# Edge scatter spread over tables, layers and dot stage, with fused products, in a graph network on one core

## The reference

```python
src, dst, edge_attr_32            # edges sorted by dst; 32 features per edge
# L0: three graph attention layers of 4 heads
e = leaky_relu(alpha_s[src] + alpha_d[dst], 0.2)
alpha = softmax over the edges of one dst;  x = relu(segment_sum(alpha * h[src], dst) + b)
# L1: GIN      mlp(segment_sum(x[src], dst) + (1 + eps) * x), normed over nodes, relu
# L2: dot      exp_s = exp(clip(q[dst] . k[src], -10, 10)); attention with v, plus x
# L3: GINE     mlp(x + segment_sum(relu(x[src] + edge_attr @ We + be), dst)), normed, relu
```

## Time and profile before

| What | us |
|---|---|
| runs, lowest to highest | 6104.78 to 6120.56 |
| median of 3 runs | 6106.02 |
| the profiled execution | 6116.9 |
| its span, first to last instruction | 6114.9 |

### The profile page before, as it was taken

One profiled execution on the slowest core, in us unless ns is written; L12 is line 12 of the kernel. 1 busy time (PEld: TensorE's weight loads), 2 busy tenths in 40 slices (PEclk: granted clock), 3 DMA queues, 4 the chain that ended last, 5 costly groups with the idle time before them and its releaser, 6 DMA issues. The chain is left out here.

```text
span 6114.9 us, 65546 instructions
## 1 busy us (share of the span) xinstructions
PE 3509.3 (57%) x23361; PEld 2157.9 (35%) x23361; DVE 4003.1 (65%) x4450; ACT 2617.0 (43%) x4140; POOL 4178.9 (68%) x3306
## 2 busy tenths in 40 slices
PE   3211111211053778876889858888758783466664
PEld 2211111211052444443445434454433331344542
DVE  2644445554377999959998599996649995233323
ACT  1000000000043777876878857788029894122211
POOL 1888888888782788846888658887001488777773
PEclk6555555555566889998989979999879997777765
DMA  8222222222397889847998569996724243323222
GB/s 284 19 19 19 21 19 4 1 1 8 41 351 244 188 211 222 183 113 175 220 220 193 108 165 221 218 216 121 261 77 143 92 128 89 109 74 79 76 52 24
DMA packets 421587, 765.52 MB, mean 125 GB/s; under 512 B 178478, under 2 KB 257197, under 8 KB 417168
## 3 DMA queue, kind: packets, MB, share of 16 engines
q0 software_dynamic: 236096, 287.22, 30.9%
q1 hardware_dynamic: 166832, 432.41, 20.5%
q10 hardware_dynamic: 18336, 41.70, 2.0%
HBM read 632.89 MB, written 128.19 MB: 124 GB/s over the span
## 5 line engine op out<-in xcount | busy, mean ns | idle before, releaser
L325 POOL DMA_INDIRECT counts<-plcell_add,plcell_slot x806 | 1255.7, 1558 | 390.5 <-issue 222.8
L1629 POOL DMA_INDIRECT emxg<-xtab,emsrc x856 | 945.5, 1105 | 454.0 <-issue 260.2
L702 ACT ACT_TABLE_LOAD x1 | 1.3, 1283 | 1614.8 <-PE mtps L690 1614.8
L417 DVE TENSOR_REDUCE plnlow<-plsame 128x13 f32<-128x1664 bf16 x62 | 117.0, 1888 | 664.6 <-DMA counts<-plcell_add,plcell_slot 664.5
L372 PE MATMUL plpsR<-plpiece,plbefore 128*128 128x500 bf16 (+1 forms) x81 | 47.1, 582 | 820.7 <-DVE plranked L502 808.0
L1210 PE MATMUL ga0psE<-ident,ga0logit 128*128 128x128 f32 x2500 | 398.4, 298 | 192.2 <-DMA ga0logit<-log_counts 168.6
L1210 PE MATMUL ga1psE<-ident,ga1logit 128*128 128x128 f32 x2500 | 401.8, 301 | 148.4 <-DMA ga1logit<-log_counts 130.9
L1210 PE MATMUL ga2psE<-ident,ga2logit 128*128 128x128 f32 x2500 | 397.2, 299 | 148.9 <-DMA ga2logit<-log_counts 117.9
L1143 ACT ACTIVATE ga0prob<-ga0psE,ga0src_fifth 128x512 f32<-128x512 f32 (+1 forms) x700 | 405.3, 672 | 146.9 <-PE ga0psE L1210 146.2
L1143 ACT ACTIVATE ga1prob<-ga1psE,ga1src_fifth 128x512 f32<-128x512 f32 (+1 forms) x700 | 405.2, 671 | 145.1 <-PE ga1psE L1210 144.4
L1143 ACT ACTIVATE ga2prob<-ga2psE,ga2src_fifth 128x512 f32<-128x512 f32 (+1 forms) x700 | 405.5, 669 | 139.4 <-PE ga2psE L1210 138.6
(11 more groups left out here) (354 smaller groups left out, 8694.8 us busy)
## 6 DMA issues: line engine op xcount, KB each, us to landing
ga0logit<-log_counts POOLq DMA_DIRECT2D x88, 512.0 KB
ga1logit<-log_counts POOLq DMA_DIRECT2D x88, 512.0 KB
ga2logit<-log_counts POOLq DMA_DIRECT2D x88, 512.0 KB
counts<-plzeros SPq DMA_DIRECT2D x32, 1250.0 KB, 32.7
mthalf<-counts SPq DMA_DIRECT2D x50, 800.0 KB, 10.3
log_counts<-mtlogs SPq DMA_DIRECT2D x25, 1600.0 KB
ga0near<-log_counts SPq DMA_DIRECT2D x50, 800.0 KB
ga1near<-log_counts SPq DMA_DIRECT2D x50, 800.0 KB
```

What stands on the lines that cost most here:

```text
L325: nc.gpsimd.indirect_dma_start(counts[w][:, :], bass.IndirectOffsetOnAxis(ap=cell_slot[:, g % 2, j:j + 1], axis=0), cell_add[:, g % 2, j:j ...
L417: step(nc.vector.reduce_sum(nlow[:], same[:], axis=AX.X))
L702: nc.scalar.activation(logs[:, n % OUTS, q, :], ps[:, u % 3, 0:BW], ACT.Ln, bias=tiny[:, 0:1], scale=math.e).then_inc(log_made, 1)
L1629: nc.gpsimd.indirect_dma_start(xg[:, h, t, :], None, xtab[:, :], bass.IndirectOffsetOnAxis(ap=src[:, g, t:t + 1], axis=0)).then_inc(gather ...
```

## The change

The scatter groups are split anew: 8 beside the tables, 14 in each layer, and the last 12 in the block of L2 and L3, ahead of GpSimd's casts. The lists of slots and ends are loaded once for each stage instead of once for each group. SyncE's 54 row loads wait for the new scatters (semaphore `scattering`). In SyncE's queue the row loads of the first five visits stand ahead of the table's stores, and the first two early loads ahead of the last three early stores. Three products become scalar_tensor_tensor: the addition of half tables, the product with the counts (which takes over the clip's minimum) and the one-hot compare.

```diff
-TABLE_GROUPS = (0, 5)
-LAYER_GROUPS = ((5, 24), (24, 43), (43, 62))
+TABLE_GROUPS = (0, 8)
+LAYER_GROUPS = ((8, 22), (22, 36), (36, 50))
+DOT_GROUPS = (50, 62)
...
-                    nc.vector.tensor_tensor(cnt[:, n % OUTS], half[:, n % RING, 0], half[:, n % RING, 1], ALU.add).then_inc(summed, 1)
+                    nc.vector.scalar_tensor_tensor(cnt[:, n % OUTS], half[:, n % RING, 0], 0.0, half[:, n % RING, 1], ALU.add, ALU.add).then_inc(summed, 1)
...
+        pool.dma_start(slot[:], edges["slot"][:, first * G:last * G]).then_inc(tables_loaded, 16)
+        pool.dma_start(ends[:], edges["ends"][:, first * G:last * G, :]).then_inc(tables_loaded, 16)
...
-            pool.dma_start(slot[:, m, :], edges["slot"][:, g * G:(g + 1) * G]).then_inc(list_loaded[m], 16)
-            pool.dma_start(ends[:, m, :, :], edges["ends"][:, g * G:(g + 1) * G, :]).then_inc(list_loaded[m], 16)
...
+        scatter, _ = edge_scatter(nc, ctx, a, edges, "dots", *DOT_GROUPS)
...
+                sp.wait_ge(scattering, 1)
                 for g in range(SORTED_GROUPS):
...
+                sp.wait_ge(src_made, SORTED_GROUPS)
+                for i in range(ROWS):
+                    load_row(i)
                 sp.dma_start(xtab[FIRST * P:NP, :].rearrange("(t p) d -> p t d", p=P), x[:, FIRST:NT, :]).then_inc(filled, 16)
...
                 for g in range(EARLY_GROUPS):
+                    if g == EARLY_GROUPS - 3:
+                        load_early(0)
+                        load_early(1)
...
                 nc.gpsimd.iota(local_id[:], pattern=[[1, P]], base=0, channel_multiplier=0, allow_small_or_imprecise_dtypes=True).then_inc(id_made, 1)
+                for _ in scatter(pool):
+                    pass
+                pool.sem_inc(scattering, 1)
...
-                        nc.vector.tensor_scalar(w, w, EXP_LOW, EXP_HIGH, ALU.max, ALU.min).then_inc(clipped, 1)
+                        nc.vector.tensor_scalar(w, w, EXP_LOW, None, ALU.max).then_inc(clipped, 1)
...
-                        nc.vector.tensor_tensor(w, w, times(HEADS - first), ALU.mult).then_inc(prob_ready, 1)
+                        nc.vector.scalar_tensor_tensor(w, w, EXP_HIGH, times(HEADS - first), ALU.min, ALU.mult).then_inc(prob_ready, 1)
...
-                    nc.vector.tensor_tensor(same[:, v % M_BUFS, :, :], local_id[:].unsqueeze(1).to_broadcast([P, CT, P]),
-                                            row[:, i % ROWS, lo:lo + CT, ED:ED + 1].to_broadcast([P, CT, P]), ALU.is_equal).then_inc(same_ready, 1)
+                    nc.vector.scalar_tensor_tensor(same[:, v % M_BUFS, :, :], local_id[:].unsqueeze(1).to_broadcast([P, CT, P]), 0.0,
+                                                   row[:, i % ROWS, lo:lo + CT, ED:ED + 1].to_broadcast([P, CT, P]), ALU.add, ALU.is_equal).then_inc(same_ready, 1)
```

More of the change, by code:

```diff
@@ L757, in edge_scatter @@
     count = last - first
-    LISTS = 4
-    slot = sb("slot", [P, LISTS, G], i32)
-    ends = sb("ends", [P, LISTS, G, 2])
+    slot = sb("slot", [P, count * G], i32)
+    ends = sb("ends", [P, count * G, 2])
     feat = sb("feat", [P, STAGES, G, ED])
     stage = sb("stage", [P, STAGES, G, RW])
-    feat_cleared, staged = (sem(n) for n in ("feat_cleared", "staged"))
-    list_loaded = [sem(f"list_loaded{k}") for k in range(LISTS)]
+    tables_loaded, feat_cleared, staged = (sem(n) for n in ("tables_loaded", "feat_cleared", "staged"))
     feat_loaded = [sem(f"feat_loaded{k}") for k in range(STAGES)]
@@ L776, in load @@
         def load(i):
-            g, k, m = first + i, i % STAGES, i % LISTS
-            pool.dma_start(slot[:, m, :], edges["slot"][:, g * G:(g + 1) * G]).then_inc(list_loaded[m], 16)
-            pool.dma_start(ends[:, m, :, :], edges["ends"][:, g * G:(g + 1) * G, :]).then_inc(list_loaded[m], 16)
+            g, k = first + i, i % STAGES
             rows = feat[:, k, :, :].rearrange("p t k -> p (t k)")
@@ L789, in steps @@
         load(0)
+        pool.wait_ge(tables_loaded, 32)
         for i in range(count):
-            k, m = i % STAGES, i % LISTS
+            k = i % STAGES
             if i + 1 < count:
                 load(i + 1)
-            pool.wait_ge(feat_loaded[k], sum(loads(n) for n in range(k, i + 1, STAGES)))
-            pool.wait_ge(list_loaded[m], 32 * (i // LISTS + 1))
+            pool.wait_ge(feat_loaded[k], sum(loads(m) for m in range(k, i + 1, STAGES)))
             if i >= STAGES:
@@ L798, in steps @@
             nc.gpsimd.tensor_copy(stage[:, k, :, 0:ED], feat[:, k, :, :]).then_inc(staged, 1)
-            nc.gpsimd.tensor_copy(stage[:, k, :, ED:RW], ends[:, m, :, :]).then_inc(staged, 1)
+            nc.gpsimd.tensor_copy(stage[:, k, :, ED:RW], ends[:, i * G:(i + 1) * G, :]).then_inc(staged, 1)
             pool.wait_ge(staged, 2 * i + 2)
[L801 to L804, removed]
+            for t in range(i * G, (i + 1) * G):
+                nc.gpsimd.indirect_dma_start(edges["sorted"][:, :], bass.IndirectOffsetOnAxis(ap=slot[:, t:t + 1], axis=0),
+                                             stage[:, k, t - i * G, :], None).then_inc(scattered[k], 16)
+                yield t
         for k in range(STAGES):
@@ L1559, in dot_and_messages @@
         flat_a = ps_a.rearrange("p k c -> p (k c)")
[L1560 to L1561 removed]
+        be_loaded, we_cleared, we_loaded, column_loaded, need_loaded, need_met, scattering, zero_made, id_made = (
+            esem(n) for n in ("be_loaded", "we_cleared", "we_loaded", "column_loaded", "need_loaded", "need_met", "scattering", "zero_made", "id_made"))
         row_loaded = [esem(f"row_loaded{k}") for k in range(ROWS)]
@@ L1588, in _, with load_early @@
                 sp.dma_start(xtab[0:FIRST * P, :].rearrange("(t p) d -> p t d", p=P), y[:, 0:FIRST, :]).then_inc(x_stored, 16)
+                def load_early(g):
+                    if g < E_BUFS:
+                        sp.wait_ge(prob_used, TILES)
+                    else:
+                        sp.wait_ge(raw_ready, visit_end[visit_of[g - E_BUFS] + 1])
+                    sp.wait_ge(early_stored[g % XG], 16 * (g // XG + 1))
+                    sp.dma_start(early_in[:, g % E_BUFS].rearrange("p k d -> p (k d)"), edges["early"][g * P:(g + 1) * P, :]).then_inc(early_loaded[g % E_BUFS], 16)
                 for g in range(EARLY_GROUPS):
+                    if g == EARLY_GROUPS - 3:
+                        load_early(0)
+                        load_early(1)
                     for c in range(NCH):
@@ L1598, in _ @@
                         sp.wait_ge(feat_packed, i - ROWS + 1)
-                    sp.dma_start(row[:, i % ROWS, :, :].rearrange("p k w -> p (k w)"), sorted_groups[g]).then_inc(row_loaded[i % ROWS], 16)
-                    if g < EARLY_GROUPS:
-                        if g < E_BUFS:
-                            sp.wait_ge(prob_used, TILES)
-                        else:
-                            sp.wait_ge(raw_ready, visit_end[visit_of[g - E_BUFS] + 1])
-                        sp.wait_ge(early_stored[g % XG], 16 * (g // XG + 1))
-                        sp.dma_start(early_in[:, g % E_BUFS].rearrange("p k d -> p (k d)"), edges["early"][g * P:(g + 1) * P, :]).then_inc(early_loaded[g % E_BUFS], 16)
+                        load_row(i)
+                    if 2 <= g < EARLY_GROUPS:
+                        load_early(g)
             @block.gpsimd
```

3 lines of the change are left out of this document (2 added, 1 removed).

## The result

The changed kernel takes 6164.41 us (median of 4 runs, 6158.69 to 6169.34), the kernel before 6107.2 beside it (4 runs): a ratio of 1.0087 with a 95% interval of 1.0069 to 1.0106. It is slower by 57 us, 0.9%; 6176 was forecast, in a range of 6062 to 6250.

A forecast was written before the change was run, and what follows sets the result against it. VectorE and GpSimd were taken as both near their limit in the layers, and GpSimd's gather chain as setting the end. Tables +25, layers −75, dot stage +120 sum to +70: 6176 us, range 6062 to 6250.

The forecast's parts named there:

- the three terms: Whole kernel: +25 us in the tables, −75 in the three layers, +120 in the dot stage, summing to +70.
- Products: Three products as scalar_tensor_tensor: same durations as before and GpSimd not freed, 0 us.
- Tables: Table stage: three more scatter groups make GpSimd finish after VectorE's last product, +25 us, bounds 0 and +50.
- Layers: Three layers: five fewer groups each return somewhat over a third of VectorE's wait, −25 us per layer, −75 in all.
- The sign named for it was too strong: Layers of about 760 us, with TensorE's waits for masks down from 96 to 60 us or so.
- Dot stage: Twelve groups ahead of the gathers: first gather 184 us late, the gather chain ends 120 us later; bounds +51 and +174.
- The next step: Dot stage: 96 gathers move to where they take 1.25 instead of 1.924 us, so 184 us delay costs 120.
- First rows and early loads: SyncE's reordered loads fill part of the other engines' 116 us stillness, but gathers set the messages' pace: 0 us.
- The sign named for it failed: Before the messages: the other engines' 116 us of stillness shorter or filled, with no effect on the end.
- GpSimd paces the layers: Layers: TensorE's mask waits come from scatters, 60 us back per layer, 6071 us; decides from 48 per layer; chance 0.15.
- The layers return nothing: Layers: mask transfers, not their issue, hold TensorE, so no gain; sum +145, 6251 us; chance 0.12.

The follow-up runs named there:

- e1_products: The kernel before with only the three products as scalar_tensor_tensor and the clip without its minimum: 6109.9 us, ratio 0.9996 to the kernel before.
- e3_tables5: The changed kernel with 5 groups beside the tables, 15 in each layer, 12 in the dot stage: 6138.7 us, ratio 1.0040 to the kernel before.
- e7_layers5: The changed kernel with lists per group, 5 groups in the tables, 5 in each layer, 42 in the dot stage: 6701.0 us, ratio 1.0961 to the kernel before.
- e5_dots6: The changed kernel with 5 groups beside the tables, 17 in each layer, 6 in the dot stage: 6049.8 us, ratio 0.9890 to the kernel before.
- e10_hold: The kernel before with SyncE's 54 row loads held until 72 of 125 dot-stage tiles are added up, no scatters there: 6204.0 us, ratio 1.0144.
- e4_old_rows: The changed kernel with SyncE's old order, first rows behind the early stores, first two early loads behind the last three: 6160.8 us, ratio 1.0079 to the kernel before.

## Why the prediction was right

The result is 12 us below the forecast, and the three terms are there with the signs that were worked out. In the two profiled executions they add up to +50 instead of +70: the dot stage was taken 29 us too dear, the tables 7 too cheap. What follows are the sizes.

*Products: 0, right*, and alone as well (e1_products). In the changed kernel they take 1498 and 834 ns, with the scatters beside them. The rule of the Trainium skill that spoke against them (Vector Engine (DVE) Microarchitecture Reference, section 7: half throughput for two SBUF sources that are not bf16) is not borne out by either trace.

*Tables: +25 forecast, 31.9 measured.* The mechanism is the one given: GpSimd is done 34 us past VectorE's last product, and e3_tables5 gave the stage back. The size was 7 us off because a group beside the products took 39.0 us, not 36.3: leaving out the list loads did not shorten it, and 6 groups fitted instead of 6.6.

*Layers: −75 forecast, −73.3 measured.* The 25 us were not worked out but chosen, at somewhat over a third of VectorE's wait, so that they fit this closely is in part luck. VectorE's wait for ScalarE shrank by 20.6 us in layer 0, and some 3 came at the layer's end, which the prediction did not look at. e7_layers5 shows that the rest of that wait does not depend on GpSimd, and the lengths by groups show where the gain ends:

| Scatter groups in a layer | layers 0, 1, 2, us |
|---|---|
| 19 (before) | 790.9, 795.7, 793.5 |
| 17 (e5_dots6) | 770.2, 774.1, 777.5 |
| 15 (e3_tables5) | 763.2, 775.3, 775.0 |
| 14 (changed) | 763.5, 772.5, 770.8 |
| 5 (e7_layers5) | 754.9, 760.9, 767.5 |

With 19 groups GpSimd has 54.5 us to spare in a layer and paces it in places; with 17 the wait has grown to 100 and most of the gain is had. (Two other kernels with the 19 groups and lists of before had 776.8 to 795.2, so a single difference below 10 us says little. The three layers together take 2361 to 2380 us in the three kernels with 19 groups and 2296 to 2307 in the four with 14 and no memsets, the changed one among them; between the two means lie 68 us.) The sign named for it was too strong: TensorE's waits fell from 96 to 77, not to 60.

*Dot stage: +120 forecast, +91 measured; the mis-sized term.* "A group is 13 × 1.924 ..., two copies at 1.30, two loads at 0.74 and 0.3, 29.4 us" took 26.0 (4515.72 to 4827.20 is 311.5 us for 12). Groups of GpSimd in this stage:

```profile
L801 POOL DMA_INDIRECT sorted_edges<-dotsstage,dotsslot x156 | 236.6, 1517 | 47.2 <-issue 43.9 <-POOL dotsstage L798 3.4
...
L797 POOL COPY dotsstage<-dotsfeat 128x416 f32<-128x416 f32 x12 | 11.0, 918 | 0.0
L783 POOL DMA_DIRECT2D dotsfeat<-in_edge_attr_dram x12 | 8.0, 667 | 7.5 <-DMA dotsends<-edge_ends 7.2 <-POOL dotsfeat L770 0.3
L798 POOL COPY dotsstage<-dotsends 128x26 f32<-128x26 f32 x12 | 7.7, 638 | 0.0
```

A scatter took 1.82 us instead of 1.924, and copies and loads, priced from layer 0, 0.6 to 0.9 us here. The 54 row loads took 57.7 instead of 63.6. So the first gather was 139 us late, not 184: 41 of the 45 are the groups. The next step held: the delay times 1.25/1.92, here and in e10_hold.

*First rows and early loads: 0, right* (e4_old_rows). The sign named for it failed: the stillness of the other engines got longer, 140 us for 116, since the gathers that the messages wait for came later than the new order could make up.

*Rivals.* "GpSimd paces the layers" was half the truth: it did, in places, with 19 groups, and for 22 to 24 us a layer, not the 48 or more from which it would have decided. "The layers return nothing" was out by 73 us.

## What to carry to other kernels

Before work is moved into an engine's idle time, ask what ends that idle time: here a wait for the norm of the first nodes covers six or seven groups, and those behind them start the chain that sets the end later. A delay of a chain that runs partly beside other work costs less than its length, by the ratio of its two paces (0.65 here), and one wait put into the old kernel measures that without the change. A gain from unloading an engine ends once that engine has time to spare, so a few units less may bring nearly all of it (here two groups less and fewer list loads, not separated).

## What was unexpected

In the first 278 us of the dot stage the granted clock was 0.88 of 2.4 GHz in the changed kernel, where scatters ran, and 0.92 before, in the mean over stretches at the higher level and shorter ones at 1.2 GHz, with TensorE as busy; the products ended 15 us later. In e10_hold, with the gathers as late but without scatters, they did not, though its clock in that window was 0.90. That window of the kernel before, and of the changed one:

```profile
4552.00:4830.00 278.00, 213.22 (x1894) 88.85 (x1894) 255.56 (x322) 242.46 (x362) 39.82 (x63) 0.92 0.41 138
```

```profile
4502.70:4780.70 278.00, 212.46 (x1798) 87.32 (x1798) 248.30 (x306) 230.08 (x345) 230.30 (x179) 0.88 0.30 96
```

What lowered the clock was not tried, and the clock alone does not explain the 15 us: e7_layers5, with scatters beside all products, had 0.91 there and ended them at 578.0.

Small GpSimd memsets that move no DMA made VectorE's one-input clamps of 1024 elements 856 ns long instead of 807.
